# Earlier loads, single peak pairs, split first rows and a lead of three in a four-layer Perceiver kernel

## The reference

```python
x = x + _L0_xattn_ref(ctx_1024, ctx_1024, _layernorm(x), ...)   # one head
x = x + _L0_attn_ref(_layernorm(x), ...)      # 16 heads, relative positions
x = x + _L0_ffn_ref(_layernorm(x), ...)       # routed experts, one per token
x = x + _L1_xattn_ref(ctx_1024, _layernorm(x), ...)             # heads of 64
x = x + _L1_attn_ref(_layernorm(x), ...)      # gated delta rule, a scan over tokens
x = x + _L1_ffn_ref(_layernorm(x), ...)       # experts with capacity
x = x + _L2_xattn_ref(_layernorm(x), ctx_1024, ctx_1024, ...)   # heads of 16
x = x + _L2_attn_ref(_layernorm(x), ...)      # causal, rotary, with its own feed-forward
x = x + _L2_ffn_ref(_layernorm(x), ...)       # experts choose tokens
x = x + _L3_xattn_ref(_layernorm(x), ctx_1024, ctx_1024, ...)   # heads of 16
x = x + _L3_attn_ref(_layernorm(x), ...)      # state-space scan
x = x + _L3_ffn_ref(_layernorm(x), ...)       # top 4 of 16 experts and a shared one
```

```python
pos_emb = dist_emb[MAX_POS - 1 + distance]
scores = scores + jnp.einsum('bqhd,qkd->bhqk', q, pos_emb)
scores = scores + jnp.einsum('bkhd,qkd->bhqk', k, pos_emb)
```

## Time and profile before

| | us |
|---|---|
| median of 3 runs | 3938.63 (3932.94 to 3941.34) |
| profiled execution | 3929.64 |
| its span, first to last instruction | 3927.8 |
| TensorE busy | 3305.8 (84%) |
| VectorE busy | 2274.1 (58%) |
| ScalarE busy | 1509.9 (38%) |
| GpSimd busy | 903.5 (23%) |
| mean granted TensorE clock | 0.921 of 2.4 GHz |
| DMA | 346.74 MB, mean 88 GB/s |

### The profile page before, as it was taken

How to read it: one execution, slowest core, us unless ns; L and a number is a source line. 1 busy time by engine, 2 the same in 40 slices (tenths; PEclk the granted TensorE clock), 3 DMA queues, 4 the chain that set the end, 5 groups by cost and what they waited for, 6 DMA issues and landing times. The chain is left out here.

```text
span 3927.8 us, 54884 instructions
## 1 busy us (share of the span) xinstructions
PE 3305.8 (84%) x20909; PEld 2024.7 (52%) x20968; DVE 2274.1 (58%) x3668; ACT 1509.9 (38%) x2233; POOL 903.5 (23%) x666
## 2 busy tenths in 40 slices
PE   6968796999999999999579396999775689994659
PEld 4835494665665656656336374444443444442225
DVE  4325314665664665655478205999562389974954
ACT  2315211433333334334256131677551146772311
POOL 1023001425425335345147012000020300000520
PEclk9969898999999999999789698999887899997879
DMA  4238552000001000000486416666003366620011
GB/s 173 102 127 272 207 219 81 6 6 4 7 1 55 9 4 7 6 1 1 133 297 233 173 44 168 128 126 131 14 19 114 88 162 127 132 50 22 0 41 43
DMA packets 228564, 346.74 MB, mean 88 GB/s; under 512 B 104016, under 2 KB 177424, under 8 KB 223696
## 3 DMA queue, kind: packets, MB, share of 16 engines
q1 hardware_dynamic: 227920, 342.16, 29.6%
q0 software_dynamic: 384, 1.05, 0.1%
HBM read 257.15 MB, written 86.02 MB: 87 GB/s over the span
## 5 line engine op out<-in xcount | busy, mean ns | idle before, releaser
L1539 DVE TENSOR_REDUCE L1x_pk<-L1x_psm 128x1 f32<-128x512 f32 (+1 forms) x576 | 374.9, 661 | 179.8 <-PE L1x_psm L1368 169.9
L1338 POOL TENSOR_TENSOR L1x_acc<-L1x_acc,L1x_pr 128x512 f32<-128x512 f32 x256 | 416.3, 1626 | 137.4 <-ACT L1x_pr L1515 119.0
L1515 ACT ACTIVATE L1x_pr<-L1x_pss 128x1024 f32<-128x1024 f32 x272 | 278.6, 1024 | 288.0 <-PE L1x_pss L1427 280.5
L1561 DVE TENSOR_TENSOR L1x_acc<-L1x_acc,L1x_pr 128x512 f32<-128x512 f32 x256 | 261.3, 1021 | 201.9 <-ACT L1x_pr L1515 197.5
L1148 DVE TENSOR_REDUCE L3x_pk<-L3x_psm 128x1 f32<-128x512 f32 x512 | 328.2, 685 | 35.2 <-PE L3x_psm L985 31.4
L1148 DVE TENSOR_REDUCE L2x_pk<-L2x_psm 128x1 f32<-128x512 f32 x512 | 328.3, 685 | 34.5 <-PE L2x_psm L985 30.6
L1125 ACT ACTIVATE L3x_pr<-L3x_pss 128x1024 f32<-128x1024 f32 x256 | 248.1, 1021 | 103.7 <-PE L3x_pss L1026 103.4
L1125 ACT ACTIVATE L2x_pr<-L2x_pss 128x1024 f32<-128x1024 f32 x256 | 248.1, 1021 | 101.8 <-PE L2x_pss L1026 101.5
L1388 PE MATMUL L1x_pss<-L1x_cT,L1x_w 128*128 128x512 f32 (+1 forms) x576 | 277.0, 571 | 3.6 <-DMA L1x_cT<-normed_context 2.7
L1427 PE MATMUL L1x_pss<-L1x_Q,L1x_K 64*128 64x256 f32 x2176 | 279.3, 376 | 0.0
L1393 PE MATMUL L1x_pss<-L1x_w,L1x_cT 128*128 128x256 f32 x1088 | 278.4, 380 | 0.8
(11 more groups left out here) (661 smaller groups left out, 5775.2 us busy)
## 6 DMA issues: line engine op xcount, KB each, us to landing
f0e_wt<-in_f_pieces SPq DMA_DIRECT2D x10, 3072.0 KB, 11.2
offset_rows<-s_rows SPq DMA_DIRECT2D x32, 768.0 KB, 5.3
L2x_KS<-L2x_key_parts SPq DMA_DIRECT2D x24, 1024.0 KB, 13.0
L3x_KS<-L3x_key_parts SPq DMA_DIRECT2D x24, 1024.0 KB, 13.1
s_add<-offset_rows SPq DMA_DIRECT2D x32, 512.0 KB, 6.6
n_cT<-in_ctxT SPq DMA_DIRECT2D x32, 512.0 KB, 4.7
f1e_wt<-in_f_pieces SPq DMA_DIRECT2D x8, 2048.0 KB, 15.0
L2x_key_parts<-n_kst SPq DMA_DIRECT2D x32, 384.0 KB, 2.8
```

What stands on the lines that cost most here:

```text
L1338: i = nc.gpsimd.tensor_tensor(acc[:, n, 1, :, :], acc[:, n, 1, :, :], pr[:, A % RING, :, 1, :], ALU.add)
L1515: nc.scalar.activation(pr[:, A % RING, :, :, :].rearrange("p h e q -> p (h e q)"), pss[:, x:x + 2, :].rearrange("p h n -> p (h n)"), ACT.E ...
L1539: nc.vector.reduce_max(pk[:, m, hq, j:j + 1], psm[:, i % 2, 0:NQ[j][1]], AX).then_inc(peak_read, 1)
L1561: i = nc.vector.tensor_tensor(acc[:, n, 0, :, :], acc[:, n, 0, :, :], pr[:, A % RING, :, 0, :], ALU.add)
```

## The change

- **Loads begun in the preceding stage.** The weights of eleven stages get tiles and semaphores in the scope that surrounds them and are issued either in the layer norm's `fetch` or in the stage before; `projection_ahead`, `latent_weights`, `attention_tables` and `rotation_ahead` allocate and issue them, and the stage that uses them gets their semaphores in `also`. That holds for the output projections (`L1p`, `dp`, `L2xp`, `s2p`, `L3xp`, `mp`), both self-attentions' projections and tables, the rotation, the bias `s2_b2`, the delta rule's and the state-space part's weights, and the last router.
- **Layer 0's start.** The norm's `fetch` issues `wq`, `wk`, `bq` and the first quarter of `cT`; the rest is issued by SP in the stage `l0q`, and the rows `V1` in the attention stage, ahead of the second batch's context.
- **Experts of layers 1 and 2.** The stage that only issues keeps one expert's weights; the others are issued at the start of the experts' stage.
- **Single peak pairs among values.** `first_values` makes half of its matmuls at a time, and the peaks' matmuls go between the halves.
- **Delta rule's first rows apart.** The first 2 of the blocks' rows get a load of their own, ahead of context chunk 0, which goes ahead of the rest; in the blocks stage chunk 0 goes ahead of the heads, and the context's weights are issued one stage earlier.
- **Three pairs ahead.** LAG is 3 in layer 0.

```diff
+class Ahead:
+    def __init__(self, t, name, loads):
+        self.here, self.need = t.sem(name + "_here"), 16 * loads
...
+def projection_ahead(t, name, d, w, chunks=KC, bias=None):
+    held = Ahead(t, name, 1 + (bias is not None))
+    held.w = t.sb(name + "_w", [P, chunks, D])
...
+    def issue(sp):
+        sp.dma_start(held.w[:, :, :], d[w]).then_inc(held.here, 16)
...
-def project_residual(nc, k, srcT, w, name, chunks=KC, bias=None):
+def project_residual(nc, k, srcT, w, name, chunks=KC, bias=None, held=None):
-    with Tensors(nc) as t, stage(nc, name + "_load", name + "_mm", name + "_sum") as (block, load, mm, summed):
+    with Tensors(nc) as t, stage(nc, name + "_load", name + "_mm", name + "_sum", also=() if held is None else (held.here,)) as (block, load, mm, summed):
...
-            pe.wait_ge(load, 32 if bias is not None else 16)
+            pe.wait_ge(here, loads)
...
                 sp.dma_start(bq[:, :], d["L0x_bq"]).then_inc(w_load, 16)
-                for x in range(4):
+                sp.dma_start(cT[:, 0, :, span[0]], d["ctxT"][0][:, :, span[0]]).then_inc(loads[0], 16)
+
+            def fetch_more(sp):
+                for x in range(1, 4):
                     sp.dma_start(cT[:, 0, :, span[x]], d["ctxT"][0][:, :, span[x]]).then_inc(loads[x], 16)
...
-                for x in range(4):
-                    sp.dma_start(V1[:, tiles[x], 0:D], d["ctx_rows"][0][:, tiles[x], :]).then_inc(rows_loads[x], 16)
...
+                @block.sync
+                def _(sp):
+                    fetch_more(sp)
...
                 for x in range(4):
+                    sp.dma_start(V1[:, tiles[x], 0:D], d["ctx_rows"][0][:, tiles[x], :]).then_inc(rows_loads[x], 16)
+                for x in range(4):
                     sp.wait_ge(loads[x], 16)
...
             for n in range(NV):
-                products(0, n * NP // NV, (n + 1) * NP // NV)
+                products(0, n * NP // NV, (2 * n + 1) * NP // NV // 2)
...
-                first_values(n)
+                first_values(n, 0)
+                products(0, (2 * n + 1) * NP // NV // 2, (n + 1) * NP // NV)
+                first_values(n, 1)
...
 def cross16(nc, k, d, pre):
-    layer_norm(nc, k, k.X, k.N, pre + "n", k.NT)
     with Tensors(nc) as t:
+        wo = projection_ahead(t, pre + "p", d, pre + "_wo4", chunks=KC * 2, bias=pre + "_bo")
+        layer_norm(nc, k, k.X, k.N, pre + "n", k.NT, fetch=wo.issue)
...
-                for e in range(RING):
-                    load_expert(sp, e)
-                sp.dma_start(Y[:, E:KT, :], d["f1_b2"]).then_inc(biased, 16)
+                load_expert(sp, 0)
...
             @block.sync
             def _(sp):
+                for e in range(1, RING):
+                    load_expert(sp, e)
+                sp.dma_start(Y[:, E:KT, :], d["f1_b2"]).then_inc(biased, 16)
                 for e in range(RING, E):
...
-                for e in range(E):
-                    sp.dma_start(wt[:, e * PER:(e + 1) * PER, :],
...
+                load_expert(sp, 0)
...
+                for e in range(1, E):
+                    load_expert(sp, e)
...
-    LAG = 4 if relative else 0
+    LAG = 3 if relative else 0
...
+            share.load(sp, 0)
             sp.dma_start(qkv[:, 1, :, :, :].rearrange("p c t e -> p (c t e)"), by_group(heads[1])).then_inc(load, 16)
...
+            rows_of(0, FEW, first_load)
+            share.load(sp, 0)
+            rows_of(FEW, PB, load[0])
             share.begin(sp)
```

## The result

| | before | after |
|---|---|---|
| median (runs) | 3939.68 us (3932.94 to 3941.34, 4) | 3850.11 us (3848.74 to 3851.52, 4) |
| profiled execution | 3929.64 us, span 3927.8 | 3848.74 us, span 3846.7 |
| TensorE busy | 3305.8 us, 84% | 3324.0 us, 86% |
| mean granted TensorE clock | 0.921 | 0.925 |
| clears of semaphores | 123 | 151 |

The changed kernel takes 0.9782 of the time before (95% interval 0.9768 to 0.9795), 89.6 us less by the medians and 80.9 by the two profiled executions: that of before lay 10 us under its median. The forecast was 3838, 100.9 less; 3850 is inside its range (3818 to 3862), 2 us outside the stretch of 3828 to 3848 that had the chance of 0.65, and as far from 3838 as from the 3862 of the rival that covers fail in part.

The account below looks back on a forecast made before the run. It took the kernel as a string of 56 stages between which all engines meet, so a load at a stage's start costs its whole latency. Gains of 112.6 less 11.7 for clears, -100.9 from 3938.63, gave 3838; range 3818 to 3862.

Parts of the forecast that it names:

- covers fail in part: Rival (0.2): layer 0's weights +2, adds +8, layer 2's experts +8, stalls in both narrow cross-attentions +6; about 3862.
- single peak pairs: Cross-attention 2 and 3, value steps: 3.51 falls to 2.6 a step; 8 us gained in each, 16 in all.
- three pairs ahead: Layer 0's relative attention: one score step of 5.6 falls away, less a wait on adds; net gain 2.3 (0 to 5.6).
- Loads moved ahead: Starts of sixteen stages: waits from SP's issue to the first user go to nothing; 52.5 gained (49 to 53).
- The two stages that only issue: Ahead of layer 1's and layer 2's experts: one expert's load left in each, the rest covered; 19.5 and 6.3 gained.
- Layer 0's start: First norm and queries: next stage starts 14.4 earlier, weights wv and wo 3 us late; gain 11 (9 to 14).
- Delta rule: Blocks stage gains 5 (2 to 6) by the earlier context chunk; chunks stage 0 (0 to 4), its stall staying.
- The clears: Ends of stages: 28 more semaphore clears, 151 for 123, at 0.42 each with nothing hiding them; +11.7 (10.6 to 14).
- the rivals built on it: Relative attention's 13 steady steps: adds late by 1 to 2, taken as +8 within "covers fail in part" (0.2).
- the one on the slower side: Rival (0.02): late adds make every steady step wait; slower only past 16 us of landing, 17.5 giving about 3955.
- the rule of the page "DMA: Bandwidth & Descriptors": Relative attention's adds land in 3.2 us, whole 5.6 gained; the adds' part of a rival at about 3825 (0.1).
- The rival that early loads would still hold SP at the norms' barriers: Rival (0.03): small waits only move ahead one stage, so the 52.5 of loads moved are gone; 3890.

Follow-up runs that it names:

- second profile: The changed kernel run again with no edit, beside the other experiments: 3853.56 us (3847.78 to 3854.51).
- The third experiment: The changed kernel with four staging buffers instead of two for the values in the narrow cross-attentions: 3833.07 us, ratio 0.9750 to the kernel before.

## Why the forecast was right, point by point

**The direction and the size** were right: 89.6 us faster by the medians, 100.9 forecast, inside the range. Without the clears the gain is 101 by these medians, 92.7 by the two profiles and 110 by the pair with one clear to a stage, against 112.6. By the table 20 of the 112.6 are missing, nearly all in two terms, the single peak pairs and the three pairs ahead. The three figures differ by as much as these runs scatter, so that the total came as near as 11 us says less than the terms do, and is in part luck.

**Loads moved ahead** (forecast 52.5): right, 52.5 over the sixteen stages (the tables' share read with four pairs ahead), and one by one to within about 2 us. Their scatter has one source that the forecast did not take in: after these waits TensorE starts at its lower clock, and how much of the stage's work it does there depends on when the clock rises again. It gave back 1.6 in layer 1's projection and gave 1.3 in the state-space output.

**The two stages that only issue** (19.5 and 6.3): 19.8 and 6.3, with a microsecond of it lost in the experts. **Layer 0's start**: 12.65 to the attention stage's start and 0.8 in it, for 11; there the weights were 1.9 late, not 3. In the second profile, with the 1.6 of lower clock, it is 11.7 in all, so of the 13.4 some 1.6 is luck. **Delta rule**: 5.6 for blocks, and 0.8 lost for chunks where the stall grew to 10.07: right.

**The clears** (+11.7): 11.6 in the trace, 28 of them. Costed from seven barriers in a row, this was the best-founded term, and the one that no reading of busy time would have shown.

**Single peak pairs** (forecast 16, measured 6.7 between first copy and first exponential: 64.74 to 60.41 and 62.84 to 60.46). The mechanism was right, VectorE was starved and no longer is, and so was the key stack as the point to which the stall is tied. Two sizes were off. The step is 2.77 and not 2.6: TensorE sets it. And I let the steps behind the stall bring their full share, while they ran on TensorE's lower clock after a stall that had grown to 11 us: from the stalled copy to the values' load it was 11.0 before and 11.8 after. The term should have been less than half of what I took. The third experiment shows that the rest, and more, was in the stall. The 0.0 in the table has two further losses. A further 1.4 and 2.9 lie between the first and the last exponential, in stops of TensorE without a releaser, of which the last section tells. And 0.8 and 1.3 lie ahead of the first value copy, which comes 4.7 after the first value matmul where it was 3.8: a pair of products now stands between the two halves of this step too, all of it at the lower clock.

**Three pairs ahead** (forecast a gain of 2.3, measured a loss of 2.3 to 2.7): the sign was wrong. The step that failed is the tail, where the forecast had a wait of 3.3 us (to 398.4 + 6.6 = 405.0) and no cost beside it. I took the landing of the adds from the median over the stage (6.6), and the second of four issues; the rows of after say 7.5 for the median, and the wait was 5.03. The pair's adds were issued at 377.50 and the score began at 386.64, 9.1 later, where my sum had 1.3 + 6.6 = 7.9. And I did not count that TensorE comes out of this wait at half clock, 2.5 us for that one step. 5.03 + 2.5 is more than the 5.6 that fell away. The steady part held, with no wait on the adds, so the rivals built on it, and the one on the slower side, fall. So does the rule of the page "DMA: Bandwidth & Descriptors" of the Trainium skill (Anatomy of one DMA) as a rival: the estimate from it was 3.2 us for these loads, where the traces have 6.6 and 7.5. The page gives that fit for DMAs on GpSimd's path, and SyncE issues these, so the forecast stretched it.

**The rivals.** That covers fail in part was the nearest: the adds' tail and the cross-attentions' stall are such cases, and they fell about 14 short of the forecast together, over half of that rival's 24. But of its four parts only the cross-attentions' came: in the steady steps the adds landed in time, and layer 0's weights and the experts' were no later than forecast. The rival that early loads would still hold SP at the norms' barriers was wrong; they cost 0.4 each and hid behind the norm.

## What to carry to other kernels

A wait at the start of a stage is worth its length in the timeline, and it can be summed over a whole program; but first ask what the bookkeeping of the new arrangement adds to every stage, here 0.43 us for each further run of semaphore numbers, which a fixed block of them takes away altogether (40 us). Where a loop's faster step runs up against a transfer that sits behind a larger one in the same queue, cost the gain only up to the point where that larger transfer is issued, and look for another buffer instead. And cost a wait of TensorE with what follows it: here, after 5.03 us of waiting, the next step took 2.5 us more.

## What the runs showed of the hardware

TensorE stops without a releaser at fixed places of the program. The clearest is in cross-attention 3 of the changed kernel, timeline of TensorE and ScalarE:

```profile
3399.35 1.05 PE L1080 MATMUL L3x_pso<-L3x_pr,L3x_V 128*17 128x256 f32 x15
...
3403.38 0.61 PE L1080 MATMUL L3x_pso<-L3x_pr,L3x_V 128*17 128x256 f32 x1 [2.98 <-issue]
...
3405.53 1.94 ACT L1170 ACTIVATE L3x_pr<-L3x_pss 128x1024 f32<-128x1024 f32 x2 [4.90 <-PE L3x_pss L1068]
```

The average's sixteenth matmul comes 2.98 us after the fifteenth with "issue" as its releaser (it waits for nothing that the profile shows), then runs at the lower clock (0.61), and ScalarE idles 4.90 before its next exponentials where 0.68 is usual. Where these stops stand changes with the number of instructions ahead of them (one clear to a stage moves them all), and the time from the first to the last of the 256 exponentials of a cross-attention differs by 1 to 7 us between kernels that do the same work there: 341.1 and 343.1 us before, 342.5 and 346.0 after, 347.4 and 350.3 with the old order.

The traces record the fetch of instructions too, as DMA queues of their own. The queues' packets, MB and share of 16 engines, between 3381 and 3400.4 us, where the queue of the loads is the only one, and between 3400.4 and 3403.4, the stop:

```profile
q1 hardware_dynamic: 530, 3.25, 80.9%
...
q8 instruction: 1, 0.02, 2.6%
q14 instruction: 1, 0.01, 1.3%
```

Among the exponentials the ten profiles have 34 stops of 0.8 us or more with "issue" as releaser. In every one a packet of q8 (16 KB) landed 1.2 to 1.7 us before TensorE went on; a moment taken at random there would have one so one time in twenty. That packet had started 17 to 22 us after the one ahead of it in its queue, where 10.1 is the median, and each time 2 to 4 loads of keys or values were in flight when it started. So these stops end with a fetch that came late beside the loads. The packets don't say which engine they are for. Nor is it shown why they are late at these places and not at others: three in four of the long intervals between fetches bring no such stop, and no run takes the loads away. The stops set a floor of some 5 us under what a single profile of this kernel can say of a change in those stages: the changed kernel's own two profiles differ by 2.8 and 1.6 there.
